# Graph attention on one core: transposed-square transfers per group of four units instead of per slot, with mixing a slot later and the projections re-timed

## The chip, the cores and the metric

The kernel runs on one core of a Trainium2 chip. The metric is device time in microseconds (us) of one execution. Besides the timed runs there is one profiled execution of the kernel before, from which all rows below are taken.

## What is computed

Eight batches of 1024 tokens with 384 features go through masked attention with six heads of 64 features, an output projection, a residual and a layer norm. All arithmetic is fp32.

```python
q = _heads(x @ Wq + bq); k = _heads(x @ Wk + bk); v = _heads(x @ Wv + bv)
scores = jnp.einsum('bhqd,bhkd->bhqk', q, k) / np.sqrt(64)
bias = jnp.where(adj, 0.0, -9e15)[:, None]
probs = jax.nn.softmax(scores + bias, axis=-1)
ctx = jnp.einsum('bhqk,bhkd->bhqd', probs, v)
out = _layernorm(x + ctx.reshape(8, 1024, 384) @ Wf + bf)
```

## The kernel before

**Units, slots, groups.** A unit is one head against one tile of 128 queries: 128 x 1024 scores. A slot holds two units, the two heads of a pair for the same query tile. A batch has 24 slots. A group is two consecutive slots (four units: two query tiles, called qt 0 and 1, of one pair of heads); a batch has 12 groups, and three groups (six slots) finish 256 queries.

**The way of one slot s.** TensorE (PE) computes the scores in line 503 from `q_hi`, `q_lo`, `k_hi`, `k_lo` (three products of fp32r halves stand for one fp32 product) into `score_ps`, which holds one slot only. VectorE (DVE) adds the mask and takes the row minimum of the negated scores (line 689), writing `prob`. ScalarE (ACT) takes the exponential and the row sum (line 611). DVE transposes 32x32 blocks inside `prob` (line 697). What is left of the transposition of the 128x1024 probabilities is a move of 32-partition strips between partitions, and DMA does that: `move_square` (line 301) copies one strip a, c from `prob` to `prob_t`. There are 16 strips: SyncE (SP) issues the 12 with a different from c, ACT issues the 4 others. When both slots of a group have landed, PE mixes: `mix` (line 519) multiplies `prob_t` with `v_all` into `context_ps`. DVE multiplies the result with the spread inverse sums (`divide`, line 707), ACT makes `context_hi`, GpSimd (POOL) makes `context_lo`.

**The table `STEADY`.** Everything else is a job in a written table, slot by slot. Its letters: x transposes the input of the next batch, k, q and v are projections, i spreads the inverse sums of a group (line 439), m mixes a group, p is an output projection of a tile of 128 tokens (lines 408 to 410). In ("q", 2, 1, 0) the numbers are the pair, the 256 queries and the batch ahead. On PE a slot is: scores of s, then its jobs in the order of the table. On ACT: two exponentials, evictions of the jobs, the four DMA issues, `context_high`. On DVE: two maskings, two transposes, `divide`, inverse sums, then for each p `add_residual` and `moments`. On POOL: the low halves of x, k and q (`low_part`, line 812), the next mask, `make_diagonal` for the next group (line 818), `context_low`, `residual` (line 801), `normalise` (lines 839 to 843, 294). Each engine runs its own list in order and waits on semaphores.

**What ties the engines.** The scores of slot s+1 wait until slot s is masked. Jobs share three banks of `job_ps`: a job waits until the job three before it has been evicted, and evictions stand behind the exponentials of their slot. The masking of a slot waits until its part of `prob` has landed in `prob_t`; `prob` has three slots (`RING = 3`). `prob_t` has two groups; the moves of a group wait until the group two before it is mixed. `context_high` reuses one of six `context_hi` buffers. The first scores of a pair wait for the low halves of its q:

```python
def scores(b, s):
    group, pair, qt = s // 6, s % 6 // 2, s % 2
    pe.wait_ge(masked, at(b, UNITS, 2 * s + 2))
    if qt == 0:
        for kind, piece in (("k", 1), ("q", group)):
            if kind == "k" and group:
                continue
            pe.wait_ge(lo_done, needed(b, kind, pair, piece))
```

Six further tables say in which slot SP stores and loads (`STORES`, `RES_LOADS`, `X_LOADS`) and POOL adds `bf` and normalises (`RESIDUALS`, `NORMALISE`).

Of the kernel before, what the change touches and what calls it, by code (L numbers as in the profile page):

```python
# [14 lines left out]
P = 128  # L15
# [7 lines left out]
SLOTS = 24  # L23
RING = 3
# [34 lines left out]
LAST_22 = [("p", 4, 0, 0), ("p", 5, 0, 0)]  # L59
LAST_24 = [("i", 11, 0, 0), ("m", 11, 0, 0), ("p", 6, 0, 0), ("p", 7, 0, 0)]  # L60
# [5 lines left out]
STORES = {5: -2, 12: -1, 16: 0, 20: 1}  # L66
RES_LOADS = {8: 2, 15: 3, 19: 0, 23: 1}
X_LOADS = {2: (0, 0), 4: (0, 1), 11: (1, 0), 14: (1, 1)}
RESIDUALS = {1: 0, 2: 1, 11: 2, 17: 3}
NORMALISE = {3: -2, 10: -1, 13: 0, 18: 1}  # L70
# [14 lines left out]
def slot_work(mode, s):  # L85

    if s >= SLOTS:
        return LAST_24 if mode == "last" else []
    if mode == "first" and s < 2:
        return FIRST_0 if s == 0 else FIRST_1  # L90
    if mode == "last" and s == 22:
        return LAST_22
    return [w for w in STEADY[s] if not (mode == "first" and w[1] < 0) and not (mode == "last" and w[3] == 1)]


def slots_of(mode):
    return range(SLOTS + 1 if mode == "last" else SLOTS)
# [8 lines left out]
def graph_attention(nc, x, adj, wq, bq, wk, bk, wv, bv, wf, bf, out):  # L106
# [15 lines left out]
    with ExitStack() as ctx:  # L122
# [16 lines left out]
        res = sb("res", [P, TT, H], F32)  # L139
# [7 lines left out]
        context_hi = sb("context_hi", [P, 2 * FT, GQ], F32R)  # L147
        context_lo = sb("context_lo", [P, 2 * FT, GQ], F32R)
# [5 lines left out]
        row_min = sb("row_min", [P, 2 * RING], F32)  # L154
# [14 lines left out]
        bv_wide = prob[:, RING - 1, 3].rearrange("p h n -> p (h n)")[:, 0:FT * P].rearrange("p (t n) -> p t n", t=FT)  # L169
# [14 lines left out]
        res_loaded = [sem(f"res_loaded{g}") for g in range(4)]  # L184
# [6 lines left out]
        landed = [sem(f"landed{i}") for i in range(RING)]  # L191
# [22 lines left out]
        stored = [sem(f"stored{g}") for g in range(4)]  # L214
# [95 lines left out]
        def _(sp):  # L310
# [6 lines left out]
            for g in (2, 3):  # L317
                sp.dma_start(res[:, 2 * g:2 * g + 2, :], x_tiles[0, :, 2 * g:2 * g + 2, :]).then_inc(res_loaded[g], 16)
# [8 lines left out]
            sp.dma_start(bf_rows[:], bf.partition_broadcast(P)).then_inc(bf_in, 16)  # L327
            for g in range(2):
                sp.dma_start(res[:, 2 * g:2 * g + 2, :], x_tiles[0, :, 2 * g:2 * g + 2, :]).then_inc(res_loaded[g], 16)
            for i in range(RING):  # L330
                sp.sem_inc(landed[i], 256)
# [7 lines left out]
            def move(b, s):  # L339
                sp.wait_ge(squared, at(b, UNITS, 2 * s + 2))  # L340
                if s % 2 == 0:
                    sp.sem_inc(sp_waited, 1)
                    sp.wait_ge(mixed, at(b, GROUPS, s // 2 + 1))
                for a in range(4):
                    for c in range(4):
                        if not (a == c):
                            move_square(sp, s, a, c)
# [12 lines left out]
            def load_residual(b, group, ahead):  # L360
                sp.wait_ge(stored[group], at(b, 16, 16 * ahead))
# [544 lines left out]
```

## Time and profile before

| | |
|---|---|
| timed runs | 1724.23, 1729.52, 1731.74 us, median 1729.52 |
| the profiled execution | 1730.58 us, of which the span of the instructions is 1728.6 |
| busy in the span | PE 77%, DVE 61%, ACT 42%, POOL 38% |
| mean granted clock of TensorE | 0.881 of full speed |
| DMA | 251.61 MB, mean 146 GB/s |

Busy time counts no DMA issues. What SP does shows only in the chain that ended last, in its waits and in its timeline.

### The profile page before, as it was taken

Reading aid. Unit: us, or ns where it says so; the run is one execution under the profiler, and the core shown is the slowest. Engines: PE = TensorE matmul, PEld = TensorE weight load, DVE = VectorE, ACT = ScalarE, POOL = GpSimd, SP = SyncE. Lnnn points to the kernel's source line nnn. Section 1 sums busy time; section 2 is a strip of 40 time slices with the busy share of each in tenths; the row PEclk is TensorE's granted clock in tenths of the full one; section 3 lists DMA queues with packets and bytes.
Section 4 is the critical chain, followed back from the end, with each engine's and each line's share of the span. In section 5 each row is a group of like instructions: output and inputs, shape, how many; then the busy total and the mean of one; then the engine's idle time right before and its main releaser. Section 6 shows DMA issues by size and latency. Waiting matters only on the chain.

```text
span 1728.6 us, 29185 instructions
## 1 busy us (share of the span) xinstructions
PE 1326.2 (77%) x8406; PEld 948.2 (55%) x8406; DVE 1060.2 (61%) x1617; ACT 721.8 (42%) x1404; POOL 655.7 (38%) x958
## 2 busy tenths in 40 slices
PE   7777887777877689677897688866887778888773
PEld 5555565545745457455574455644656545565542
DVE  5566665765656656565566765566656567566752
ACT  5444543444434444344443434434443435443430
POOL 2223542444414444154432543325433245333333
PEclk9888898889988889897998888988899889998877
DMA  4556655565455655555555555565555555555552
GB/s 152 141 132 154 159 143 147 150 160 153 121 152 147 163 147 131 147 150 155 147 136 152 149 151 141 138 156 152 149 145 138 154 153 150 153 133 153 149 144 74
DMA packets 184872, 251.61 MB, mean 146 GB/s; under 512 B 52464, under 2 KB 86384, under 8 KB 184688
## 3 DMA queue, kind: packets, MB, share of 16 engines
q1 hardware_dynamic: 147824, 199.06, 44.1%
q10 hardware_dynamic: 36864, 50.38, 11.9%
q8 instruction: 80, 1.31, 0.4%
q14 instruction: 104, 0.85, 0.2%
HBM read 35.33 MB, written 12.58 MB: 28 GB/s over the span
## 4 chain that ended last, share of the span: by engine, by line
SPq 79%; issue 9%; PE 4%; ACT 2%; DVE 2%; DMA 2%; ACTq 1%; POOL 1%; POOLq 0%; DVEq 0%
SPq L301 76%; PE context_ps L519 2%; DMA prob_t<-prob 1%; ACT prob L611 1%; DVE prob L697 1%; ACTq L301 1%; SPq L371 1%; PE score_ps L503 1%; SPq L357 1%; SPq L336 1%; SPq L364 1%; PE job_ps L408 0%; DMA x_in<-in_x_dram 0%; POOL res L294 0%; DVE weight_lo L758 0%
## 5 line engine op out<-in xcount | busy, mean ns | idle before, releaser
L519 PE MATMUL context_ps<-prob_t,v_all 128*64 128x256 f32 x3072 | 468.4, 472 | 239.8 <-DMA prob_t<-prob 239.8
L611 ACT ACTIVATE prob<-prob,row_min 128x1024 f32<-128x1024 f32 x384 | 439.5, 1146 | 500.1 <-DVE row_min L689 433.6
L689 DVE CUSTOM_DVE_ANT_0 prob<-score_ps,mask 128x1024 f32<-128x1024 f32 x384 | 454.3, 1220 | 206.1 <-PE score_ps L503 168.4
L697 DVE STREAM_TRANSPOSE prob<-prob 128x1024 f32<-128x1024 f32 x384 | 457.9, 1231 | 148.9 <-ACT prob L611 148.9
L519 PEld LDWEIGHTS context_ps<-prob_t,v_all 128*64 128x64 f32 x3072 | 294.6, 173 | 413.8 <-issue 298.3
L818 POOL TENSOR_TENSOR diag<-ident,inv_sum 128x512 f32<-128x512 f32 x96 | 99.9, 1040 | 410.5 <-DVE inv_sum L702 408.8
L619 ACT ACTIVATE context_hi<-context 128x256 fp32r<-128x256 f32 x96 | 40.1, 418 | 456.1 <-DVE context L707 285.2
L812 POOL TENSOR_TENSOR q_lo<-raw,q_hi 128x256 fp32r<-128x256 f32 x95 | 69.4, 730 | 351.0 <-ACT raw L603 350.9
L707 DVE TENSOR_TENSOR context<-context_ps,context 128x256 f32<-128x256 f32 x96 | 40.0, 416 | 238.1 <-PE context_ps L519 237.9
L408 PE MATMUL job_ps<-xt_hi,weight_hi 128*128 128x256 f32 (+1 forms) x423 | 149.4, 353 | 26.9 <-ACT raw L601 26.7
L503 PE MATMUL score_ps<-k_hi,q_hi 64*128 64x512 f32 x768 | 145.0, 456 | 21.8 <-DVE row_min L689 16.4
L410 PE MATMUL job_ps<-xt_hi,weight_lo 128*128 128x256 f32 (+1 forms) x423 | 137.2, 324 | 0.0
L409 PE MATMUL job_ps<-xt_lo,weight_hi 128*128 128x256 f32 (+1 forms) x423 | 137.0, 324 | 0.0
L503 PE MATMUL score_ps<-k_lo,q_hi 64*128 64x512 f32 x768 | 123.8, 400 | 0.0
L503 PE MATMUL score_ps<-k_hi,q_lo 64*128 64x512 f32 x768 | 122.2, 395 | 0.0
L408 PEld LDWEIGHTS job_ps<-xt_hi,weight_hi 128*128 128x128 f32 x423 | 81.0, 191 | 74.0 <-issue 36.7
L439 PE MATMUL job_ps<-diag,ones 128*64 128x256 f32 x384 | 68.2, 436 | 52.3 <-POOL diag L818 52.3
L294 POOL TENSOR_SCALAR res<-res,mean_var,inv_dev 128x384 f32<-128x384 f32 x64 | 105.0, 1647 | 6.9 <-POOL inv_dev L843 6.9
L824 POOL TENSOR_TENSOR context_lo<-context,context_hi 128x256 fp32r<-128x256 f32 x96 | 70.5, 735 | 95.2 <-ACT context_hi L619 94.7
L503 PEld LDWEIGHTS score_ps<-k_hi,q_hi 64*128 64x128 f32 x768 | 59.4, 192 | 84.8 <-issue 61.8
L812 POOL TENSOR_TENSOR k_lo<-raw,k_hi 128x512 fp32r<-128x512 f32 x46 | 58.3, 1287 | 110.4 <-ACT raw L603 110.4
L410 PEld LDWEIGHTS job_ps<-xt_hi,weight_lo 128*128 128x128 f32 x423 | 81.3, 192 | 6.7
(72 smaller groups left out, 1717.7 us busy)
## 6 DMA issues: line engine op xcount, KB each, us to landing
prob_t<-prob SPq DMA_DIRECT2D x2304, 64.0 KB, 2.0
prob_t<-prob ACTq DMA_DIRECT2D x768, 64.0 KB, 2.1
res<-in_x_dram SPq DMA_DIRECT2D x32, 384.0 KB, 3.7
out_dram<-res SPq DMA_DIRECT2D x32, 384.0 KB, 2.5
x_in<-in_x_dram SPq DMA_DIRECT2D x30, 384.0 KB, 3.5
adj_in<-in_adj_dram SPq DMA_DIRECT2D x31, 256.0 KB, 2.8
prob_t<-in_L_gnn_Wk_dram SPq DMA_DIRECT2D x1, 576.0 KB, 3.9
prob_t<-in_L_gnn_Wq_dram SPq DMA_DIRECT2D x1, 576.0 KB, 7.8
```

Of the source, the lines that this page charges most:

```text
L294: engine.tensor_scalar(res[:, n, :], res[:, n, :], mean_var[:, group % 2, tile, 0:1], inv_dev[:, group % 2, tile:tile + 1], ALU.subtract, ...
L301: queue.dma_start(prob_t[32 * c:32 * c + 32, group % 2, qt, a].rearrange("p h n -> p (h n)"), prob[32 * a:32 * a + 32, ring, c].rearrange( ...
L408: pe.matmul(dst, left_hi, right_hi, start=(t == 0), stop=False)
L409: pe.matmul(dst, left_hi, right_lo, start=False, stop=False)
L410: last = pe.matmul(dst, left_lo, right_hi, start=False, stop=(t == FT - 1))
L503: last[head] = pe.matmul(score_ps[:, head, keys], q_part[rows, pair, q], k_part[rows, pair, keys], start=(n == 0), stop=(n == 2))
L519: last = pe.matmul(context_ps[64 * head:64 * head + 64, 0:GQ], v_all[:, kt, col:col + HS], keys, start=(kt == 0), stop=(kt == TT - 1))
L611: nc.scalar.activation(probabilities(t), probabilities(t), ACT.Exp, scale=-1.0, bias=row_min[:, ring:ring + 1], accum_out=row_sum[:, s // ...
L689: nc.vector.tensor_tensor_reduce(probabilities(t), in_quarters(score_ps[:, head, :]), in_quarters(mask[:, s % 2, :]), 1.0, HUGE, ALU.add, ...
L697: nc.vector.transpose(probabilities(t), probabilities(t)).then_inc(squared, 1)
L812: nc.gpsimd.tensor_tensor(lo, copy[:, 0:width], hi, ALU.subtract).then_inc(lo_done, 1)
L818: nc.gpsimd.tensor_tensor(diag[:], ident[:].unsqueeze(1).to_broadcast([P, 4, P]), inv_sum[:, group % 2, :].unsqueeze(2).to_broadcast([P, 4 ...
```

## The change

- `prob` becomes [partition, 2 groups, 4, 2 query tiles, 2 heads, 256], and `prob_t` [partition, 2 groups, 4, 2 query tiles, 2 heads, 256] with the query tile inside. So a strip of one group is 32 partitions with one run of 4 KB each. `move_square` takes a group: 16 issues for two slots where 32 stood. `move` stands in odd slots only, and waits for all four units of the group.
- The masking of a slot waits for landed data in even slots only, four slots after the buffer was last filled.
- Mixing moves: groups 0 to 3 from slots 5, 6, 7, 9 to 6, 8, 9, 10; groups 4 to 9 one slot later, to 12, 14, 16, 18, 20, 22; groups 10 and 11 to slots 0 and 2 of the next batch (from 23 and 1). Projections stand mostly in odd slots.
- `res` shrinks from 8 tiles to 4, `context_hi` and `context_lo` from 6 buffers to 4, with other waits on `stored`, `projected` and `res_loaded`. `context_high` of group g now waits for the projections that read group g-4.
- The last batch has two slots of leftovers instead of one.

```diff
 STEADY = {
-    12: [("q", 1, 2, 0), ("p", 1, 0, 0)],
-    13: [("i", 5, 0, 0), ("m", 5, 0, 0)],
-    14: [("q", 2, 2, 0)],
-    15: [("i", 6, 0, 0), ("m", 6, 0, 0)],
+    12: [("i", 4, 0, 0), ("m", 4, 0, 0)],
+    13: [("q", 1, 2, 0), ("p", 1, 0, 0)],
+    14: [("i", 5, 0, 0), ("m", 5, 0, 0)],
+    15: [("q", 2, 2, 0), ("q", 0, 3, 0), ("p", 2, 0, 0)],
...
-RESIDUALS = {1: 0, 2: 1, 11: 2, 17: 3}
-NORMALISE = {3: -2, 10: -1, 13: 0, 18: 1}
+RESIDUALS = {2: -1, 10: 0, 14: 1, 20: 2}
+NORMALISE = {0: -2, 8: -1, 14: 0, 18: 1}
...
-        prob = sb("prob", [P, RING, 4, 2, GQ], F32)
-        prob_t = sb("prob_t", [P, 2, 2, 4, 2, GQ], F32)
+        prob = sb("prob", [P, 2, 4, 2, 2, GQ], F32)
+        prob_t = sb("prob_t", [P, 2, 4, 2, 2, GQ], F32)
...
-        def move_square(queue, s, a, c):
-
-            group, qt, ring = s // 2, s % 2, s % RING
-            queue.dma_start(prob_t[32 * c:32 * c + 32, group % 2, qt, a].rearrange("p h n -> p (h n)"),
-                            prob[32 * a:32 * a + 32, ring, c].rearrange("p h n -> p (h n)")
-                            ).then_inc(landed[ring], 16)
+        def move_square(queue, group, a, c):
+
+            queue.dma_start(prob_t[32 * c:32 * c + 32, group % 2, a].rearrange("p q h n -> p (q h n)"),
+                            prob[32 * a:32 * a + 32, group % 2, c].rearrange("p q h n -> p (q h n)")
+                            ).then_inc(landed[group % 2], 16)
...
-            def move(b, s):
-                sp.wait_ge(squared, at(b, UNITS, 2 * s + 2))
-                if s % 2 == 0:
-                    sp.sem_inc(sp_waited, 1)
-                    sp.wait_ge(mixed, at(b, GROUPS, s // 2 + 1))
+            def move(b, group):
+                sp.wait_ge(squared, at(b, UNITS, 4 * group + 4))
+                sp.sem_inc(sp_waited, 1)
+                sp.wait_ge(mixed, at(b, GROUPS, group + 1))
...
-                for s in (2 * group, 2 * group + 1):
-                    pe.wait_ge(landed[s % RING], at(b, 256 * SLOTS // RING, 256 * (s // RING + 2)))
+                pe.wait_ge(landed[group % 2], at(b, 128 * GROUPS, 256 * (group // 2 + 2)))
...
             def context_high(b, group):
                 act.wait_ge(context_done, at(b, GROUPS, group + 3))
-                if group % 3 == 0:
-                    act.wait_ge(projected, at(b, TT, 2 * (group // 3) + 2))
-                nc.scalar.activation(context_hi[:, group % 6, :], context[:], ACT.Copy).then_inc(context_hi_done, 1)
+                act.wait_ge(projected, at(b, TT, 2 * ((group - 4) // 3) + 6))
+                nc.scalar.activation(context_hi[:, group % 4, :], context[:], ACT.Copy).then_inc(context_hi_done, 1)
...
                 if head == 0:
-                    dve.wait_ge(landed[s % RING], at(b, 256 * SLOTS // RING, 256 * (s // RING + 1)))
+                    if s % 2 == 0:
+                        dve.wait_ge(landed[s // 2 % 2], at(b, 128 * GROUPS, 256 * (s // 4 + 1)))
```

Order of instructions on SP, at the head of the loop over the middle batches, slots 0 and 1 of the kernel before. A move of 12 strips is the row that waits and the row x11.

```order
L343 ISA [waits squared]
L301 DMA prob_t<-prob 32x512 [waits mixed]
L301 DMA prob_t<-prob 32x512 x11
L340 REGISTER_ALU
L301 DMA prob_t<-prob 32x512 [waits squared]
...
L336 ISA [waits mask_done]
L336 DMA adj_in<-in_adj_dram 128x2x1024
```

The same place in the changed kernel, slots 0 and 1:

```order
L338 ISA [waits squared]
L298 DMA prob_t<-prob 32x1024 [waits mixed]
L298 DMA prob_t<-prob 32x1024 x11
L330 ISA
L332 ISA [waits mask_done]
L332 DMA adj_in<-in_adj_dram 128x2x1024
```

The move of slot 0 is gone, and that of slot 1 carries 32x1024 elements per issue instead of 32x512.

Order on POOL before, from slot 12 on: the low half of q (pair 1, third 256 queries), in slot 13 the diagonal and `context_lo` around group 5 and `normalise` (its twelve small instructions shortened to the first), in slot 14 the low half of q (pair 2, third 256 queries).

```order
L812 TENSOR_TENSOR q_lo<-raw,q_hi 128x256 [waits job_out]
...
L818 TENSOR_TENSOR diag<-ident,inv_sum 128x512 [waits job_done]
L824 TENSOR_TENSOR context_lo<-context,context_hi 128x256 [waits context_hi_done]
...
L839 TENSOR_TENSOR newton<-inv_dev 128x2 [waits guess_done]
...
L294 TENSOR_SCALAR res<-res,mean_var,inv_dev 128x384 [waits root_ops]
L294 TENSOR_SCALAR res<-res,mean_var,inv_dev 128x384
...
L812 TENSOR_TENSOR q_lo<-raw,q_hi 128x256 [waits job_out]
```

After, from slot 13 on: low half of the same q, in slot 14 diagonal, `context_lo`, `residual`, `normalise`, in slot 15 the low halves of two q.

```order
L798 TENSOR_TENSOR q_lo<-raw,q_hi 128x256 [waits job_out]
...
L804 TENSOR_TENSOR diag<-ident,inv_sum 128x512 [waits job_done]
L810 TENSOR_TENSOR context_lo<-context,context_hi 128x256 [waits context_hi_done]
L787 TENSOR_TENSOR res<-res,bf_rows 128x384 [waits res_loaded1]
L787 TENSOR_TENSOR res<-res,bf_rows 128x384
...
L825 TENSOR_TENSOR newton<-inv_dev 128x2 [waits guess_done]
...
L292 TENSOR_SCALAR res<-res,mean_var,inv_dev 128x384 [waits root_ops]
L292 TENSOR_SCALAR res<-res,mean_var,inv_dev 128x384
L798 TENSOR_TENSOR q_lo<-raw,q_hi 128x256 [waits job_out] x2
```

The residual stands ahead of `normalise` now, and the q of pair 2 is made in slot 15 instead of 14; its scores stay in slot 16.

## Rows read from the trace of the kernel before

**Rows 1.** The page: busy time, share, instructions; the chain that ended last.

```profile
PE 1326.2 (77%) x8406; PEld 948.2 (55%) x8406; DVE 1060.2 (61%) x1617; ACT 721.8 (42%) x1404; POOL 655.7 (38%) x958
...
SPq 79%; issue 9%; PE 4%; ACT 2%; DVE 2%; DMA 2%; ACTq 1%; POOL 1%; POOLq 0%; DVEq 0%
```

**Rows 2.** The page: DMA queue of ACT; issues of the moves, size, time to landing.

```profile
q10 hardware_dynamic: 36864, 50.38, 11.9%
...
prob_t<-prob SPq DMA_DIRECT2D x2304, 64.0 KB, 2.0
```

**Rows 3.** Waits of SP: who for whom, total us, times, longest.

```profile
SPq L369 <- POOL res L294: 22.2, 2, 15.6
```

**Rows 4.** Timeline of SP's queue: start, us, instructions merged.

```profile
916.57 0.38 SPq L357 DMA_DIRECT2D x_in<-in_x_dram  x1
917.06 7.52 SPq L301 DMA_DIRECT2D prob_t<-prob  x12
```

**Rows 5.** Windows of 210 us: busy of PE, PEld, DVE, ACT, POOL, clock, DMA share.

```profile
1110.00:1320.00 210.00, 165.20 (x1050) 117.49 (x1049) 129.27 (x200) 88.44 (x173) 82.97 (x120) 0.89 0.58 148
```

**Rows 6.** Timeline of PE: scores, spread, mix, scores, q, p, scores.

```profile
746.36 0.73 PE L503 MATMUL score_ps<-k_hi,q_hi 64*128 64x512 f32 x4
...
747.95 0.65 PE L439 MATMUL job_ps<-diag,ones 128*64 128x256 f32 x4
750.60 3.67 PE L519 MATMUL context_ps<-prob_t,v_all 128*64 128x256 f32 x32 [2.00 <-DMA prob_t<-prob]
754.20 0.74 PE L503 MATMUL score_ps<-k_hi,q_hi 64*128 64x512 f32 x4
...
755.79 0.39 PE L408 MATMUL job_ps<-xt_hi,weight_hi 128*128 128x256 f32 x1
...
756.98 0.34 PE L408 MATMUL job_ps<-weight_hi,context_hi 128*128 128x384 f32 x1
...
758.64 0.73 PE L503 MATMUL score_ps<-k_hi,q_hi 64*128 64x512 f32 x4
```

**Rows 7.** Timeline of DVE: a masking, the first p, the next masking.

```profile
721.65 1.23 DVE L689 CUSTOM_DVE_ANT_0 prob<-score_ps,mask 128x1024 f32<-128x1024 f32 x1 [1.17 <-PE score_ps L503]
...
726.62 0.52 DVE L714 TENSOR_TENSOR res<-job_ps,res 128x384 f32<-128x384 f32 x1
...
730.14 1.22 DVE L689 CUSTOM_DVE_ANT_0 prob<-score_ps,mask 128x1024 f32<-128x1024 f32 x1 [0.17 <-issue]
```

**Rows 8.** Timeline of ACT: the eviction of a q behind both exponentials.

```profile
725.21 0.45 ACT L596 ACTIVATE q_hi<-job_ps,bias_qk 128x256 fp32r<-128x256 f32 x1
```

**Rows 9.** Timeline of PE and DVE in a slot with five jobs.

```profile
736.97 0.72 PE L503 MATMUL score_ps<-k_hi,q_hi 64*128 64x512 f32 x4
...
738.84 1.23 DVE L689 CUSTOM_DVE_ANT_0 prob<-score_ps,mask 128x1024 f32<-128x1024 f32 x1 [1.16 <-PE score_ps L503]
...
743.51 0.39 PE L408 MATMUL job_ps<-xt_hi,weight_hi 128*128 128x256 f32 x1 [3.43 <-ACT raw L601]
```

**Rows 10.** Timeline of POOL: a q_lo, a residual; start and end of normalise.

```profile
1641.54 0.73 POOL L812 TENSOR_TENSOR q_lo<-raw,q_hi 128x256 fp32r<-128x256 f32 x1 [6.40 <-ACT raw L603]
...
1646.51 1.96 POOL L801 TENSOR_TENSOR res<-res,bf_rows 128x384 f32<-128x384 f32 x2
...
1651.12 0.19 POOL L839 TENSOR_TENSOR newton<-inv_dev 128x2 f32<-128x2 f32 x1
...
1654.88 3.28 POOL L294 TENSOR_SCALAR res<-res,mean_var,inv_dev 128x384 f32<-128x384 f32 x2 [0.22 <-POOL inv_dev L843]
```

**Rows 11.** Timeline of PE: a mix after a long wait.

```profile
783.13 5.18 PE L519 MATMUL context_ps<-prob_t,v_all 128*64 128x256 f32 x32 [5.96 <-DMA prob_t<-prob]
```

**Rows 12.** Head and tail: first scores; last moves of ACT; last mix.

```profile
25.14 0.74 PE L503 MATMUL score_ps<-k_hi,q_hi 64*128 64x512 f32 x4
...
1693.24 2.45 ACTq L301 DMA_DIRECT2D prob_t<-prob  x4
...
1704.54 5.28 PE L519 MATMUL context_ps<-prob_t,v_all 128*64 128x256 f32 x32 [6.70 <-DMA prob_t<-prob]
```

More of the change, by code:

```diff
@@ L23 @@
 SLOTS = 24
-RING = 3
 STEADY = {
[24 rows of a table removed]
[24 rows of a table added]
 }
@@ L87, in slot_work @@
     if s >= SLOTS:
-        return LAST_24 if mode == "last" else []
+        return LAST_24 if s == SLOTS else LAST_25
     if mode == "first" and s < 2:
         return FIRST_0 if s == 0 else FIRST_1
-    if mode == "last" and s == 22:
-        return LAST_22
     return [w for w in STEADY[s] if not (mode == "first" and w[1] < 0) and not (mode == "last" and w[3] == 1)]
 def slots_of(mode):
-    return range(SLOTS + 1 if mode == "last" else SLOTS)
+    return range(SLOTS + 2 if mode == "last" else SLOTS)
 MODES = ("first", "mid", "last")
@@ L183, in graph_attention @@
         x_loaded = [sem(f"x_loaded{i}") for i in range(2)]
-        res_loaded = [sem(f"res_loaded{g}") for g in range(4)]
+        x_early = sem("x_early")
+        res_loaded = [sem(f"res_loaded{i}") for i in range(2)]
         adj_loaded = sem("adj_loaded")
@@ L190, in graph_attention @@
         squared = sem("squared")
-        landed = [sem(f"landed{i}") for i in range(RING)]
+        landed = [sem(f"landed{i}") for i in range(2)]
         inverted = sem("inverted")
@@ L213, in graph_attention @@
         pool_waited = sem("pool_waited")
-        stored = [sem(f"stored{g}") for g in range(4)]
+        stored = [sem(f"stored{i}") for i in range(2)]
         def at(b, per, plus):
@@ L327, in _ @@
             sp.dma_start(bf_rows[:], bf.partition_broadcast(P)).then_inc(bf_in, 16)
+            sp.wait_ge(job_done, 6)
             for g in range(2):
                 sp.dma_start(res[:, 2 * g:2 * g + 2, :], x_tiles[0, :, 2 * g:2 * g + 2, :]).then_inc(res_loaded[g], 16)
-            for i in range(RING):
-                sp.sem_inc(landed[i], 256)
+                sp.sem_inc(landed[g], 256)
             def load_adjacency(b, group):
@@ L346, in move @@
                         if not (a == c):
-                            move_square(sp, s, a, c)
+                            move_square(sp, group, a, c)
             def load_x(b, half, i):
@@ L382, in body @@
                         store(b, STORES[s])
-                    if s in RES_LOADS:
-                        group = RES_LOADS[s]
-                        if group >= 2 and b.mode != "first":
-                            load_residual(b, group, 0)
-                        if group < 2 and b.mode != "last":
-                            load_residual(b, group, 1)
+                    if s in RES_LOADS and (RES_LOADS[s] >= 2 or b.mode != "first"):
+                        load_residual(b, RES_LOADS[s])
             body(Batch("first", 0, 0))
@@ L396, in _ @@
                 store(last, group)
-            for g in range(4):
-                sp.wait_ge(stored[g], 16 * BATCH)
+            for i in range(2):
+                sp.wait_ge(stored[i], 32 * BATCH)
         @block.tensor
@@ L416, in transpose_x @@
                 for i in range(4):
-                    src = x_in[:, i] if mode != "start" or half == 0 else res[:, 4 + i]
+                    src = x_in[:, i] if mode != "start" or half == 0 else res[:, i]
                     last = pe.transpose(bank[:, i * P:(i + 1) * P], src[:, t * P:(t + 1) * P], ident[:])
@@ L448, in project_out @@
                 three_products(job_bank(b.mode, job)[:, 0:H], [
-                    (context_hi[:, 3 * (group % 2) + t, tok], context_lo[:, 3 * (group % 2) + t, tok],
+                    (context_hi[:, (3 * group + t) % 4, tok], context_lo[:, (3 * group + t) % 4, tok],
                      weight_hi[:, 3, t, :], weight_lo[:, 3, t, :]) for t in range(FT)]).then_inc(projected, 1)
@@ L538, in _ @@
                 if n == 3:
-                    for g in (2, 3):
-                        pe.wait_ge(res_loaded[g], 16)
+                    pe.wait_ge(x_early, 16)
                 if n >= 4:
@@ L607, in exponential @@
                 s, head = t // 2, t % 2
-                ring = 2 * (s % RING) + head
+                ring = 2 * (s % 4) + head
                 col = 2 * head + s % 2
@@ L627, in move @@
                         if a == c:
-                            move_square(act, s, a, c)
+                            move_square(act, group, a, c)
             def body(b):
@@ L638, in body @@
                             evict(b, job)
-                    if s < SLOTS:
-                        move(b, s)
+                    if s < SLOTS and s % 2 == 1:
+                        move(b, s // 2)
                     for job in work:
@@ L796, in residual @@
             def residual(b, g):
-                pool.wait_ge(res_loaded[g], at(b, 16, 16))
-                if g >= 2 and b.mode == "first":
-                    pool.wait_ge(job_done, 6)
-                for n in (2 * g, 2 * g + 1):
+                pool.wait_ge(res_loaded[g % 2], at(b, 32, 16 * (g // 2 + 1)))
+                for n in (2 * g % 4, 2 * g % 4 + 1):
                     nc.gpsimd.tensor_tensor(res[:, n, :], res[:, n, :], bf_rows[:], ALU.add).then_inc(res_done, 1)
@@ L823, in context_low @@
                 pool.wait_ge(context_hi_done, at(b, GROUPS, group + 1))
-                nc.gpsimd.tensor_tensor(context_lo[:, group % 6, :], context[:], context_hi[:, group % 6, :],
+                nc.gpsimd.tensor_tensor(context_lo[:, group % 4, :], context[:], context_hi[:, group % 4, :],
                                         ALU.subtract).then_inc(context_lo_done, 1)
@@ L854, in body @@
                         next_mask(b, s // 6 + 1, s % 6 - 4)
-                    if s == 1 and b.mode == "first":
+                    if s == 2 and b.mode == "first":
                         make_diagonal(b, 0)
@@ L862, in body @@
                             context_low(b, job[1])
-                    if s in RESIDUALS:
+                    if s in RESIDUALS and (RESIDUALS[s] >= 0 or b.mode != "first"):
                         residual(b, RESIDUALS[s])
+                    if s == SLOTS:
+                        residual(b, 3)
                     if s in NORMALISE and (NORMALISE[s] >= 0 or b.mode != "first"):
                         normalise(b, NORMALISE[s])
-                    if s == SLOTS and b.mode == "last":
+                    if s == SLOTS:
                         normalise(b, 2)
+                    if s == SLOTS + 1:
                         normalise(b, 3)
```

58 lines of the change are left out of this document (28 added, 30 removed), and 40 rows, old and new, of the table STEADY.

## The prediction

> **What bounds the kernel now.** I read the chain that ended last first: SP's queue holds 79% of it, while the busiest engine is PE at 77% and DVE has 61% [rows 1]. Next, does SP wait? Its longest entry is 22.2 us in two waits in the whole span [rows 3]. So SP issues nearly all the time. Twelve issues of moves take 7.52 us, 0.63 each, after a load that occupies the queue from 916.57 to 917.06 [rows 4]. One batch is 210 us: a window of that length holds 1050 matmuls [rows 5], and one batch has 288 for scores, 384 for mixing, 48 spreads, 24 transposes and 306 in projections, 1050 together. SP's 24 moves of a batch take 24 x 7.6 = 182 us, its 16 loads and stores about 0.9 us each with what surrounds them, 15 us, and some 13 us are issues that took longer and waits: 210. The bound is the number of SP's issues, 8.75 us per slot.
>
> The other engines wait for it. PE had 5.96 us of waiting for a landed group ahead of one mix, and 6.70 ahead of the last [rows 11, 12].
>
> **The issues.** A middle batch keeps 12 moves of 12 issues on SP. If an issue of 128 KB costs what one of 64 KB does, they take 12 x 7.6 = 91 us, with the rest 91 + 15 + 6 = 112 us per batch. Can it? The bound from below is 0.38 us, what the queue is busy with a load of 384 KB in many more runs [rows 4]; from above it is cost by bytes, 1.27 us. I take 0.63: the load is six times as large and its issue is no longer, so bytes don't set it. ACT's four issues stand once per two slots instead of once per slot.
>
> SP is then far from being the bound, and what is late next is the loop of PE, DVE, ACT and POOL. It decides the time, so I add it up.
>
> **PE slot by slot.** From a stretch in which the matmuls ran fast [rows 6]: scores 1.6 us (746.36 to 747.95; 754.20 to 755.79), mix 3.6 (750.60 to 754.20), q 1.2 (755.79 to 756.98), p 1.6 (756.98 to 758.64, with some 0.1 before the scores). A v has the form of a p, 1.6. By columns k is two q's less the start, estimated 2.1, a spread is 0.5, an x 0.5. The scores of the next slot also wait for this slot's masking: the masking begins 1.9 us after the scores (736.97 to 738.84) [rows 9], and two take 2.4 us, so no slot is under 4.3. DVE needs 5.0 us from masking to the end of the transposes (721.65 to 726.62) and 3.5 for two p with moments (726.62 to 730.14) [rows 7]; a divide about 0.4.
>
> A mixing slot costs PE 1.6 + 0.5 + 3.6 = 5.8 and DVE 5.4. The ten pure ones (2, 6, 8, 9, 10, 12, 14, 16, 18, 20) give 58. Slots 0 and 22 have a q too, 6.9 each. Of the others, PE's sum and DVE's: slot 1 4.3 and 5.1, slot 3 6.4 and 5.1, slot 4 7.9, slot 5 6.4, slot 7 5.9 and 8.4, slot 13 4.3 and 7.1, slot 15 5.4 and 6.6, slot 19 5.9, slots 21 and 23 7.5 each. Slots 11 and 17 have five and six jobs for three banks, so the fourth waits for an eviction behind both exponentials. ACT reached a q's eviction 3.6 us after the masking began (721.65 to 725.21) and takes some 0.9 for it [rows 7, 8]. Before, a slot with three x, a q and a p cost 9.4 us (736.97 to 746.36), 3.43 of it that wait [rows 6, 9]. Slot 11 has these jobs, 9.3; slot 17 one more q, 10.1. Slot 4's fourth job waits 0.9 the same way; it is in the 7.9.
>
> PE's sums give 152 us per batch. Taking the longer of PE and DVE in each slot gives 160. The truth lies between, since a slot long on DVE can lend to a mixing slot. I take 156.
>
> **Waits that the new places add.**
> - *POOL behind the late q.* The scores of slot 16 need the low half of the q of pair 2, now made in slot 15. In slot 14 masking begins at 1.9, the transposes end at 6.9, divide, `context_high` and `context_lo` add 0.4, 0.4 and 0.7: 8.4 us into the slot. Then `residual`, 1.96, and `normalise`, 7.0 (1651.12 to 1658.16) [rows 10]: 17.4. The q_lo, 0.73, ends at 18.1, while PE would start slot 16's scores at 5.8 + 6.6 = 12.4. Price 5.7 us. Before, `normalise` stood one slot earlier and that q in slot 14, two slots ahead of its scores.
> - *POOL behind normalise in slot 8.* The two p of slot 7 shift DVE, so `context_lo` of group 1 ends about 10.6 us into slot 8, `normalise` at 17.6, the diagonal for group 3 at 18.7. Its spread in slot 10 is wanted at 14.0. Price 4.6. The data of group 3 comes about then too: its moves wait for mix 1.
> - *ACT in slot 12.* `context_high` of group 4 now waits for the second p, which PE does in slot 13, and the exponentials of slot 13 stand behind it: 1.7 us late. The q of slot 13 then has its low half 8.8 us into the slot, and the scores of slot 14 wait for it; PE alone would be there at 4.4, DVE at 7. Beyond the 156 this is 3.5.
>
> Together 14: 170 us per batch.
>
> **Does the data land in time?** The 12 issues take 7.6 us and the last lands 2.0 us later [rows 2]. The engines moved ACT's 50.38 MB in 11.9% of the span, 245 GB/s; a burst of 2.1 MB needs 8.6 us by that. So a group lands 9.6 to 10.6 us after its transposes. A mix two slots later is wanted some 13 us after them. Hidden, with 3 us to spare, except for groups 2 and 3, whose moves wait for the mixes of 0 and 1 in slots 6 and 8; there masking or mixing waits 0 to 1 us, beside the POOL wait counted. SBUF — State Buffer of the Trainium skill, section "Door 1: The DMA port swizzle", states that 32 partitions reach only 8 of the 16 ports, 218 GB/s. By that rule alone a burst would take 9.6 us and land at 11.6, still under 13, and cost at most 1 us in group 3, 8 us in all. The rows show 245 GB/s for strips of 32 partitions, so I keep that.
>
> **The clock.** At 0.881 granted on average, and 0.89 in a middle batch [rows 5], the clock was at its lower level, 1.2 instead of 2.4 GHz, for a quarter of the time. After a wait of 5.96 us a mix took 5.18 us, after 2.00 us 3.67 [rows 6, 11]. Three waits of 4 to 7 us remain per batch by the list above, against one ahead of most mixes today, so at 1.5 to 2.5 us each about 7. That gives 177 us per batch.
>
> **The sum.** The head is 25 us to the first scores, unchanged. Eight batches are 8 x 177 = 1416. The first lacks two p and two mixes, the last the x, k and q of a next one, worth -16. Before, the last transposes ended at 1693.2, and the span at 1728.6: 35. SP's backlog, which held the last mix until 1704.54 [rows 12], becomes one landing of 10, and `normalise` of group 2 runs ahead, so 31. 25 + 1416 - 16 + 31 = 1456 of span, against 1728.6. The profiled execution took 1730.58, 2 more than its span and 1 over the median of 1729.52. Forecast 1458 us.
>
> **Rivals.**
> - *The added waits don't come about*, since DVE's long slots delay PE anyway: 156 to 162 per batch and less low clock. 25 + 8 x 158 - 16 + 31 = 1304. For it: PE does 138 us of fast matmuls per batch. Against it: the waits are in the order and the durations in the rows. 0.13.
> - *The issue or the landing grows with bytes, in part.* At 1.0 to 1.2 us per issue a burst lands at 14 to 17 us, over the 13, and PE waits 1 to 3 us at most mixes: 183 to 198 per batch, 1510 to 1620. The same holds if PE's clock stays low for 40% of the time. For it: the runs double, both queues ask for 400 GB/s in a burst and get 245. 0.11.
> - *Slower than before: an issue of 4 KB runs costs twice or more.* The place is SP's queue. It decides from 1.27 us per issue, where 144 x 1.27 + 27 = 210 as now; at 1.4 a batch is 229, and the time 1728 + 8 x 19 = 1880. For it speaks nothing but that no row has such an issue. 0.03.
> - *No change*: the cost lies exactly at that point. 0.01.
>
> TensorE: Matmul & The Clock Gate of the Trainium skill, section "Part 1: The HAM clock gate", says that the throttled clock is the default and activity releases it. If a busier PE kept the full level throughout, the sum would lose the 7 us per batch, about 1402, inside my range.
>
> **Chances.** The forecast, 165 to 190 per batch, has 0.72. To leave out 2 in 10, the range goes to 1370 below, past which lies most of the first rival, and to 1560 above, half way through the second. Under 0.5%, 9 us, a measurement of this kernel can't be told from no change. Faster 0.96, same 0.01, slower 0.03.
>
> **What would show it.** Right: SP's queue under 15% of the chain; an issue of 128 KB at 0.55 to 0.65 us; landing within 3 us; PE waiting for POOL's q_lo ahead of one in 24 scores, about 5 us; slots 11 and 17 unchanged in length; DVE and PE sharing the chain. Wrong: issues over 1 us, PE waiting for landed data ahead of most mixes, or a batch near 158 us with no wait for POOL. The prediction fails most likely in the sum of small hand-overs between engines, which I took from few rows.

## The result and the profile after

The changed kernel takes 1574.99 us (median of 4, 1573.23 to 1576.45) against 1727.85 (median of 4, 1724.23 to 1731.74). The ratio is 0.9115, 95% interval 0.9091 to 0.9138: faster by 153 us. The forecast was 1458 us with a range of 1370 to 1560. Direction and bound were right, the time was 117 us too low, and it lies outside the range. Times are of executions in the faster of a kernel's two states; of all the runs below one execution was slow, 1532.95 us of the kernel with one `normalise` later, and it is left out of that kernel's time.

The page of the changed kernel: busy time of each engine, ACT's DMA queue, and the moves (count, size of one, us to landing).

```profile
PE 1277.9 (81%) x8406; PEld 916.7 (58%) x8406; DVE 1058.4 (67%) x1617; ACT 722.5 (46%) x1404; POOL 657.1 (42%) x958
...
q10 hardware_dynamic: 18432, 50.36, 13.1%
...
prob_t<-prob SPq DMA_DIRECT2D x1152, 128.0 KB, 3.6
prob_t<-prob ACTq DMA_DIRECT2D x384, 128.0 KB, 4.0
```

The instruction counts are those of [rows 1]; PE is busy 48 us less, since it runs at the lower clock less often. Half as many moves carry the same bytes [rows 2], and one lands after 3.6 or 4.0 us, not 2.0.

Waits in its trace: who waited for whom, total us, times, longest.

```profile
SPq L337 <- DVE prob L685: 490.4, 96, 23.8
SPq L298 <- PE context_ps L509: 80.6, 23, 5.7
...
DVE prob L685 <- ACT prob L600: 194.1, 192, 8.1
PE score_ps L494 <- POOL q_lo L798: 87.1, 17, 7.3
PE job_ps L431 <- POOL diag L804: 13.6, 7, 2.8
PE context_ps L509 <- DMA prob_t<-prob: 9.9, 2, 7.5
```

SP, whose longest entry was 22.2 us in two waits [rows 3], now waits 571 us for transposes and mixes. PE waits for landed data twice in the span. In the place of SP's queue stand waits between engines; the one to look at is DVE's for the exponentials, 194.1 us, which the forecast has no line for. It is not new, though. The same group on the page of the kernel before:

```profile
L697 DVE STREAM_TRANSPOSE prob<-prob 128x1024 f32<-128x1024 f32 x384 | 457.9, 1231 | 148.9 <-ACT prob L611 148.9
```

A middle batch of the new kernel is 191 us, not 177 (first scores of the batches at 595.4 and 786.2). Fourteen us in each of eight batches are 112 of the 117 that are missing. Its window, columns as in [rows 5]:

```profile
595.40:786.20 190.80, 158.53 (x1050) 113.18 (x1050) 130.54 (x200) 90.03 (x176) 82.99 (x120) 0.91 0.67 163
```

**Slot by slot.** I took the time from the first score matmul of each slot to that of the next, in the six middle batches, and the median of the six. "Forecast" is the prediction's own list, the longer of PE and DVE, with its three waits of POOL and ACT in their places, which comes to 173.8 (before its 7 us for the clock and the 4 that DVE lends).

| slots | forecast | after | difference |
|---|---|---|---|
| 0 to 5 | 38.5 | 44.2 | +5.7 |
| 6 to 9 | 25.8 | 36.2 | +10.4 |
| 10 | 10.4 | 7.6 | -2.8 |
| 11, 12 | 15.1 | 15.0 | -0.1 |
| 13, 14 | 16.4 | 17.0 | +0.6 |
| 15, 16 | 18.1 | 20.1 | +2.0 |
| 17 | 10.1 | 11.2 | +1.1 |
| 18 to 23 | 39.4 | 39.9 | +0.5 |

So most slots stand as worked out, and the place to look at is slots 6 to 9. Timeline of slots 6 to 8 of a middle batch, ACT, DVE, both queues and the mixes 0 and 2:

```profile
641.81 1.22 DVE L677 CUSTOM_DVE_ANT_0 prob<-score_ps,mask 128x1024 f32<-128x1024 f32 x1 [1.45 <-PE score_ps L494]
641.94 3.62 PE L509 MATMUL context_ps<-prob_t,v_all 128*64 128x256 f32 x32
...
645.61 3.73 ACTq L298 DMA_DIRECT2D prob_t<-prob  x4
...
649.45 1.15 ACT L600 ACTIVATE prob<-prob,row_min 128x1024 f32<-128x1024 f32 x1 [8.98 <-issue]
...
650.84 2.38 DVE L685 STREAM_TRANSPOSE prob<-prob 128x1024 f32<-128x1024 f32 x2 [6.65 <-ACT prob L600]
...
652.15 0.44 PE L400 MATMUL job_ps<-weight_hi,context_hi 128*128 128x384 f32 x1 [2.11 <-ACT context L575]
...
662.10 3.75 ACTq L298 DMA_DIRECT2D prob_t<-prob  x4
...
665.96 1.15 ACT L600 ACTIVATE prob<-prob,row_min 128x1024 f32<-128x1024 f32 x1 [8.14 <-issue]
...
670.16 5.36 PE L509 MATMUL context_ps<-prob_t,v_all 128*64 128x256 f32 x32 [1.95 <-DVE context L695]
```

The masking of slot 6 starts at 641.81 and lets the exponential start some 1.25 us later, at 643.1. It starts at 649.45, 6.4 us late. In between ACT's queue waits for mix 0, which ends at 645.56, and then issues four transfers until 649.34. The gap reads "issue", since an engine whose own queue waits for a semaphore shows no releaser; the row of ACTq shows what was in front. The same stands at mix 1: ACTq at 662.10, the exponential of slot 8 at 665.96, 2.7 us late. After that everything is late in turn: transposes by 6.65, the second p of slot 7 by 2.11 (it wants ACT's eviction), mix 2 by 1.95, and that mix then takes 5.36 us for 3.62.

How late ACT starts an exponential behind its masking can be read for every slot. Medians of the six middle batches: 6.4 us in slot 6, 2.7 in slot 8, 2.1 in slot 2, and 1.2, 1.1 and 1.0 in slots 10, 4 and 20, all behind ACT's moves; 1.7 in slot 13, behind `context_high`; under 0.1 us in all others. The kernel before had such a stall too. In its slot 5, in a middle batch, ACT's moves of slot 4 waited for mix 0, and the exponential began 5.2 us behind its masking:

```profile
693.19 2.46 ACTq L301 DMA_DIRECT2D prob_t<-prob  x4
...
695.76 1.15 ACT L611 ACTIVATE prob<-prob,row_min 128x1024 f32<-128x1024 f32 x1 [7.72 <-issue]
```

So the cause stood in the trace on which the forecast was made.

### The profile page after: what moved, and what is told of

Read it like the earlier page. It is cut to its first block and busy times, and to the rows that moved or that the text cites. A ratio compares the mean times of both kernels' runs of the same rounds, so it can differ in the third digit from the quotient of the medians.

```text
span 1574.4 us, 27551 instructions
## 1 busy us (share of the span) xinstructions
PE 1277.9 (81%) x8406; PEld 916.7 (58%) x8406; DVE 1058.4 (67%) x1617; ACT 722.5 (46%) x1404; POOL 657.1 (42%) x958
## 3 DMA queue, kind: packets, MB, share of 16 engines
q10 hardware_dynamic: 18432, 50.36, 13.1%
## 5 line engine op out<-in xcount | busy, mean ns | idle before, releaser
L600 ACT ACTIVATE prob<-prob,row_min 128x1024 f32<-128x1024 f32 x384 | 439.7, 1146 | 595.4 <-DVE row_min L677 439.2
L685 DVE STREAM_TRANSPOSE prob<-prob 128x1024 f32<-128x1024 f32 x384 | 458.0, 1231 | 194.1 <-ACT prob L600 194.1
L509 PE MATMUL context_ps<-prob_t,v_all 128*64 128x256 f32 x3072 | 386.6, 409 | 37.7 <-DVE context L695 27.8
L509 PEld LDWEIGHTS context_ps<-prob_t,v_all 128*64 128x64 f32 x3072 | 241.4, 150 | 177.5 <-issue 71.9
L494 PE MATMUL score_ps<-k_hi,q_hi 64*128 64x512 f32 x768 | 154.1, 481 | 148.8 <-POOL q_lo L798 87.1
L400 PE MATMUL job_ps<-xt_hi,weight_hi 128*128 128x256 f32 (+1 forms) x423 | 145.1, 343 | 0.0
L494 PE MATMUL score_ps<-k_hi,q_lo 64*128 64x512 f32 x768 | 133.0, 425 | 0.0
L494 PE MATMUL score_ps<-k_lo,q_hi 64*128 64x512 f32 x768 | 131.8, 422 | 0.0
L775 POOL TENSOR_SCALAR mask<-adj_in 128x1024 f32<-128x1024 uint8 x64 | 67.1, 1049 | 93.4 <-DVE row_min L677 58.2
L400 PE MATMUL job_ps<-weight_hi,context_hi 128*128 128x384 f32 x192 | 74.3, 387 | 21.9 <-ACT context L575 14.9
L494 PEld LDWEIGHTS score_ps<-k_hi,q_lo 64*128 64x128 f32 x768 | 80.5, 204 | 19.0
L494 PEld LDWEIGHTS score_ps<-k_lo,q_hi 64*128 64x128 f32 x768 | 80.4, 204 | 19.1
```

The costliest lines, as they stand in the source:

```text
L400: pe.matmul(dst, left_hi, right_hi, start=(t == 0), stop=False)
L494: last[head] = pe.matmul(score_ps[:, head, keys], q_part[rows, pair, q], k_part[rows, pair, keys], start=(n == 0), stop=(n == 2))
L509: last = pe.matmul(context_ps[64 * head:64 * head + 64, 0:GQ], v_all[:, kt, col:col + HS], keys, start=(kt == 0), stop=(kt == TT - 1))
L600: nc.scalar.activation(probabilities(t), probabilities(t), ACT.Exp, scale=-1.0, bias=row_min[:, ring:ring + 1], accum_out=row_sum[:, s // ...
L685: nc.vector.transpose(probabilities(t), probabilities(t)).then_inc(squared, 1)
```

## The experiments

The explanation to be tested: **ACT's issues for groups 2 and 3 wait for mixes 0 and 1, and the exponentials of slots 6 and 8 are queued behind them.** Its rivals: the transfers themselves are late (a burst lands later than forecast), or POOL's waits cost more than was counted. Each expectation names its own theories, A first. All ratios are against the kernel before on the same chip, whose medians there were 1724.93 us (first four) and 1725.21 us (last four). These lie 3 us under the 1727.85 beside which the changed kernel was timed, so that differences in us between kernels are good to some 3 us.

**ACT's issues of groups 2 and 3 behind the exponentials.**

```diff
+LATE_MOVES = (2, 3)
-                    if s < SLOTS and s % 2 == 1:
+                    if s < SLOTS and s % 2 == 1 and s // 2 not in LATE_MOVES:
                         move(b, s // 2)
+                    if s < SLOTS and s % 2 == 0 and s // 2 - 1 in LATE_MOVES:
+                        move(b, s // 2 - 1)
```

> Edit: in ACT's list the four issues of groups 2 and 3 stand after the exponentials and evictions of the next slot (6 and 8), not ahead of them; nothing else moves. Theory A (the missing time of slots 6 to 9 is ACT's: its issues wait for mix 0 and mix 1, and the exponentials queue behind them, 6.4 and 3 us late): the transposes of slot 6 end some 7 us after its scores begin instead of 13.4, slots 7 to 9 together shrink from 30 us to 21 to 25, and the kernel takes 1575 - 8 x 6 to 8 x 9, 1505 to 1530 us. Theory B (landing is the limit there: groups 2 and 3 land 13 us after mixes 0 and 1 whatever ACT does, since landing takes 3.6 us and not 2.0): masking of slots 8 and 10 then waits for the DMA instead, and the gain is under 3 us per batch, 1550 to 1575 us.

Measured: 1517.23 us (1512.62 to 1519.43), ratio 0.879 (0.8767 to 0.8812), 58 us under the changed kernel. Its slot 6, and PE in its slot 10:

```profile
618.81 1.15 ACT L601 ACTIVATE prob<-prob,row_min 128x1024 f32<-128x1024 f32 x1 [2.61 <-DVE row_min L680]
...
620.20 2.39 DVE L688 STREAM_TRANSPOSE prob<-prob 128x1024 f32<-128x1024 f32 x2 [0.28 <-ACT prob L601]
...
621.35 3.74 ACTq L299 DMA_DIRECT2D prob_t<-prob  x4
...
647.95 0.65 PE L432 MATMUL job_ps<-diag,ones 128*64 128x256 f32 x4 [4.43 <-POOL diag L807]
...
648.44 5.31 PE L510 MATMUL context_ps<-prob_t,v_all 128*64 128x256 f32 x32
```

The same four transfers now stand behind the exponentials, and the transposes wait 0.28 us where they waited 6.65. Slot 7 falls from 10.5 to 6.0, slot 9 from 11.6 to 6.7. Slot 10 grows from 7.6 to 11.8: PE waits 4.43 us for POOL's diagonal, at the place and near the 4.6 us that the forecast gave. In the changed kernel ACT's stall had covered it. Theory A holds. ACT's smaller delays, in slots 2, 4 and 20, are left as they were, and one of 1.1 us is new in slot 7.

**All sixteen issues on SP**, none on ACT.

```diff
-                        if not (a == c):
-                            move_square(sp, group, a, c)
+                        move_square(sp, group, a, c)
...
-                    if s < SLOTS and s % 2 == 1:
-                        move(b, s // 2)
```

> Edit: all 16 issues of a group on SP, none on ACT. Theory A (ACT's waiting and its 3.0 to 3.7 us of issuing per group hold back exponentials in every odd slot; SP has 40% of its time free): exponentials of slots 6 and 8 are on time, odd slots lose up to 1 us; the group lands 3 us later, at 15 us after its transposes, which eats part: 1500 to 1545 us. Theory B (landing time binds): mixes and maskings wait for the DMA, 1570 to 1640 us.

Measured: 1496.56 us (1494.77 to 1502.01), ratio 0.8683 (0.8662 to 0.8703), 78 us under the changed kernel and below what A gave. Its page and SP's queue:

```profile
prob_t<-prob SPq DMA_DIRECT2D x1536, 128.0 KB, 2.4
```

```profile
664.65 11.12 SPq L298 DMA_DIRECT2D prob_t<-prob  x16
...
678.73 10.07 SPq L298 DMA_DIRECT2D prob_t<-prob  x16
```

Sixteen issues alone take 10.07 to 11.12 us, 0.63 to 0.70 each, and land after 2.4. That is about the forecast's issue price; beside ACT's queue it was not met. Slots 6 to 9 come to 27.4 us (forecast 25.8), and slots 0 to 5 fall from 44.2 to 40.4, since ACT now starts its exponentials on time in every slot but 13. That is why this edit gives more than the one before. The last data of a group lands 12.4 us after the group's first issue, where it took 11.4 (medians of the middle batches). DVE pays 39.3 us for landed data, and it is still the better kernel.

**The new table with transfers of 64 KB**, on the two queues as after, twice as many issues.

```diff
-            queue.dma_start(prob_t[32 * c:32 * c + 32, group % 2, a].rearrange("p q h n -> p (q h n)"),
-                            prob[32 * a:32 * a + 32, group % 2, c].rearrange("p q h n -> p (q h n)")
+            for qt in range(2):
+                queue.dma_start(prob_t[32 * c:32 * c + 32, group % 2, a, qt].rearrange("p h n -> p (h n)"),
+                                prob[32 * a:32 * a + 32, group % 2, c, qt].rearrange("p h n -> p (h n)")
```

> Edit: the changed kernel's table and buffers, but each strip goes in two issues of 64 KB with runs of 2 KB, so 32 issues per two slots as before. Theory A (SP's issue count was the bound and its halving is the whole gain): SP again issues all the time, 24 x 7.6 + 15 + waits for the moves that now come in one block per group, so 1730 to 1850 us, no faster than before. Theory B (the later mixing and the odd-slot projections brought a good part of the 153 us): 1600 to 1700 us.

Measured: 1785.68 us (1777.74 to 1790.12), ratio 1.0332 (1.0305 to 1.036). Chain by engine, two waits, and the moves:

```profile
SPq 64%; PE 14%; issue 10%; ACTq 4%; DVE 3%; ACT 2%; DMA 1%; POOL 1%; DVEq 0%; POOLq 0%
```

```profile
DVE prob L678 <- DMA prob_t<-prob: 158.4, 47, 7.4
PE context_ps L510 <- DMA prob_t<-prob: 111.4, 29, 9.9
```

```profile
prob_t<-prob SPq DMA_DIRECT2D x2304, 64.0 KB, 2.0
prob_t<-prob ACTq DMA_DIRECT2D x768, 64.0 KB, 2.1
```

The new table and buffers, with one move for a whole group, cost 3.3% by themselves; only with half the issues does the change win, and it then wins 211 us over this version. The gain is the count of issues, as forecast. The old table with large transfers was not run.

**`normalise` of the first 256 queries and its store one slot later** (out of the way of the q_lo that slot 16 needs).

```diff
-STORES = {4: -2, 10: -1, 16: 0, 20: 1}
+STORES = {4: -2, 10: -1, 17: 0, 20: 1}
-NORMALISE = {0: -2, 8: -1, 14: 0, 18: 1}
+NORMALISE = {0: -2, 8: -1, 15: 0, 18: 1}
```

> Edit: normalise of group 0 (of 256 queries) in slot 15 behind the low halves of q, instead of in slot 14 ahead of them; its store one slot later, in 17. Theory A (slot 15's 11.6 us are POOL's: the q_lo that the scores of slot 16 need waits behind normalise): slot 15 falls to 7 to 8 us, slot 16 loses its slow mix too (8.5 to 6), 1575 - 8 x 5 to 8 x 6.5, 1523 to 1535 us. Theory B (ACT's eviction of that q is late anyway): under 2 us per batch, 1560 to 1575.

Measured: 1515.51 us (1503.58 to 1517.5), ratio 0.882 (0.8769 to 0.887): 59 us under the changed kernel by the median times, 51 by the ratios, with 9 us of uncertainty. The wait in the changed kernel, a row of its timeline, and what all waits for q_lo come to in this one (87.1 before the edit):

```profile
725.95 1.41 POOL L798 TENSOR_TENSOR q_lo<-raw,q_hi 128x256 fp32r<-128x256 f32 x2
726.73 1.22 PE L494 MATMUL score_ps<-k_hi,q_hi 64*128 64x512 f32 x4 [5.99 <-POOL q_lo L798]
```

```profile
PE score_ps L494 <- POOL q_lo L798: 49.3, 17, 4.4
```

The forecast had 5.7 us for this wait; it is 5.99. Slot 15 falls from 11.6 to 7.1 and slot 16 from 8.5 to 5.6, 7.4 together: the wait, and the slow matmuls behind it (scores 1.22 for 0.74). Theory A. The profiled execution is the fastest of this kernel, so that its slots show the gain at its largest; that the gain exceeds what A gave is not clear of the scatter.

**Both together.** All issues on SP, and `normalise` of the first 256 queries later, in one kernel.

```diff
-                        if not (a == c):
-                            move_square(sp, group, a, c)
+                        move_square(sp, group, a, c)
+STORES = {4: -2, 10: -1, 17: 0, 20: 1}
+NORMALISE = {0: -2, 8: -1, 15: 0, 18: 1}
```

> Edit: all 16 issues on SP and normalise of group 0 in slot 15 with its store in 17, together. Theory A (two separate stalls, ACT's queue in slots 6 to 9 and POOL's in 14 to 16): the gains of 78 and 58 us add, less what one median hides, 1430 to 1450 us. Theory B (both take up the same slack of one loop): no better than the better of the two, 1480 to 1500 us.

Measured: 1445.55 us (1444.48 to 1450.92), ratio 0.8372 (0.8352 to 0.8391). Alone the edits are worth 78 and 51 to 59 us, together 129: a sum within the scatter, two separate costs.

**Then `normalise` of the last 256 queries of the batch before one slot later too.**

```diff
-STORES = {4: -2, 10: -1, 17: 0, 20: 1}
+STORES = {4: -2, 11: -1, 17: 0, 20: 1}
-NORMALISE = {0: -2, 8: -1, 15: 0, 18: 1}
+NORMALISE = {0: -2, 9: -1, 15: 0, 18: 1}
```

> Edit: as e5_sp_and_normalise, and normalise of group 3 (of the batch before) in slot 9 instead of 8, its store in 11. Theory A (slot 10's 10.6 to 11.8 us in the kernels without ACT's stall are PE waiting for the diagonal of group 3, behind normalise on POOL, 4.6 us by the prediction): slot 10 falls to 6 to 7 us, 25 to 35 us less than e5_sp_and_normalise. Theory B (slot 10 waits for group 3's data, whose moves wait for mix 1): within 10 us of e5_sp_and_normalise, and the trace shows PE's mix waiting for the DMA there.

Measured: 1422.44 us (1420.08 to 1423.78), ratio 0.8235 (0.8215 to 0.8256), 23 us less. Slot 10 falls from 11.6 to 6.8, the 4.8 us of the diagonal. Slots 2 and 14 give back 1.6 and 1.0 of it, so the gain is a little under A's.

**Then `context_high` and `context_lo` of group 4 behind slot 13's work.**

```diff
-                        if job[0] == "m":
+                        if job[0] == "m" and job[1] != 4:
                             context_high(b, job[1])
+                    if s == 13:
+                        context_high(b, 4)
```

POOL has the same edit with `context_low(b, 4)`.

> Edit: as e6_normalise_9, and context_high and context_low of group 4 in slot 13 behind the evictions and low halves, instead of in slot 12 ahead of the exponentials of 13. Theory A (the 1.7 us by which slot 13's exponentials are late carry to the scores of slot 14, 8.8 us into the slot): slot 13 falls from 8.8 to 7.1 us, 10 to 18 us less than e6_normalise_9. Theory B (the q of slot 13, made one slot ahead of its scores, sets it alone): under 5 us.

Measured: 1405.29 us (1399.84 to 1405.4), ratio 0.813 (0.8105 to 0.8155), 17 us less: slot 13 from 8.8 to 7.2, and slots 14 and 2 give back the 1.0 and 1.6 that they had grown by in the run before (slot 4 grows by 1.4). This was the forecast's third wait. A window of 168 us of this kernel, its DVE waits and its chain:

```profile
600.00:768.00 168.00, 148.80 (x1060) 108.76 (x1056) 131.49 (x201) 91.22 (x179) 83.06 (x120) 0.98 0.77 186
```

```profile
DVE prob L684 <- ACT prob L599: 53.9, 192, 0.6
DVE prob L676 <- DMA prob_t<-prob: 44.1, 20, 3.4
```

```profile
PE 56%; issue 15%; SPq 12%; ACT 6%; DVE 5%; DMA 3%; POOL 2%; DVEq 0%; ACTq 0%; POOLq 0%
```

It is the fastest version of the study, 18.7% under the kernel before and 10.8% under the changed one. PE is what is left. It is busy 148 us with a batch's matmuls, where the changed kernel needs 159, at a granted clock of 0.98 there.

**The mixes back in the odd slots**, with the large transfers (of groups 5 to 9, spread and mix at the end of the slot before).

```diff
-    15: [("q", 2, 2, 0), ("q", 0, 3, 0), ("p", 2, 0, 0)],
-    16: [("i", 6, 0, 0), ("m", 6, 0, 0)],
+    15: [("q", 2, 2, 0), ("q", 0, 3, 0), ("p", 2, 0, 0), ("i", 6, 0, 0), ("m", 6, 0, 0)],
+    16: [],
```

> Edit: the changed kernel with spread and mix of groups 5 to 9 one slot earlier, at the end of the odd slots 13 to 21; all else as it is. Theory A (a group lands 12 to 13 us after its transposes, with 3.6 us of landing, so mixing a slot earlier meets data that are 1 to 5 us late): PE waits for the DMA ahead of five mixes per batch, 8 x 5 x 2 to 8 x 5 x 4 more, 1650 to 1730 us. Theory B (the mixes' place is nearly free once the issues are halved, since PE reaches them only behind the odd slots' projections): 1550 to 1610 us.

Measured: 1614.02 us (1608.34 to 1615.37), ratio 0.9344 (0.9314 to 0.9374), 39 us over the changed kernel.

```profile
DVE context L695 <- PE context_ps L509: 180.2, 45, 12.7
PE context_ps L509 <- DMA prob_t<-prob: 11.9, 3, 9.3
PE score_ps L494 <- POOL q_lo L798: 4.6, 8, 2.7
```

Theory A, that the mixes would wait for landed data, fell: PE waits for it 11.9 us in three waits. The loss is in the full odd slots, 17 (15.5 for 11.2), 19 (12.2 for 6.0) and 21 (11.6 for 7.6). There the mix stands behind all projections, and DVE's `divide`, and with it what DVE has next, waits for it, 180.2 us where it was 27.2. The even slots 14, 16, 20 and 22, now without a mix, win back 3.5, 3.8, 1.2 and 2.2 us. Part of that has another cause: PE's waits for q_lo fall from 87.1 to 4.6 us, so the 39 us are what is left after a second stall is gone. So in this kernel the mix's new place is not needed for the data's sake. That its gain is that the two kinds of slot are level fits these rows, but no run separates it from the waits for q_lo.

## Why the prediction was right and where it was wrong

**The bound and what removed it: right.** SP's queue was the bound, and its issues halved freed it; with the same table and issues of 64 KB it holds 64% of the chain again.

**The step that failed** stands in "Does the data land in time?": moves of groups 2 and 3 "wait for the mixes of 0 and 1 in slots 6 and 8; there masking or mixing waits 0 to 1 us". It asked when the data lands and not what stands behind the waiting issues. On SP only other transfers are queued behind them. On ACT the exponentials of the next slot are: in both kernels ACT's moves stand at the end of a slot, ahead of them. The forecast had at most 8 us for these waits in the whole span. Putting the issues of groups 2 and 3 behind the exponentials gave 58, taking all issues off ACT 78. In batches: 10 of the 14 us that a middle batch is too long are gone then (191.1 to 180.9), and the other 4 are in the terms below. The Trainium skill says of the other way to issue a DMA, from GpSimd, in DMA: Bandwidth & Descriptors, section "Anatomy of one DMA — SWDGE (gpsimd) path": "any semaphore wait happens on the issuing sequencer before dispatch". The trace agrees for ACT's issues, with 6.4 us at the first of the two.

**The added waits: right in place, near in size.** POOL behind the late q: 5.7 forecast, 5.99 measured. POOL behind `normalise` in slot 8: 4.6 and 4.43, but visible only once ACT's stall was gone, so the changed kernel does not pay for it in full (at most 2.8 us per wait). ACT in slot 12: 3.5 forecast; PE waited 4.29 for the q_lo ahead of slot 14. Slot 13 took the 8.8 us that the forecast's own account gives; what was not counted is that slot 14 then took 8.2 instead of 5.8, its mix 3.70 to 4.80 us instead of 3.62. Undoing the three waits gave 51 to 59, 23 and 17 us. The rival without them, 1304 us, is excluded; with all of them and ACT's stall gone the kernel takes 1405. Its "138 us of fast matmuls per batch" has no row: at a granted clock of 0.98 they took 148. In the second wait the spread is put at 14.0 us, where 5.8 + 5.8 + 1.6 of the forecast's own list give 13.2.

**Terms mis-sized.** Slots 0 to 5 were 5.7 us short. Of these 3.8 are the failed step again, since they go when ACT issues nothing: in slot 2 the exponentials were 2.1 us late. In slot 4 I took 7.9 us for the fourth job's wait behind the exponentials; the slot takes 10.3, and 8.3 to 9.9 in the six faster versions (11.3 before). In slot 0 the masking begins 5.8 us after the scores and not 1.9; of a wait of 3.68 us ahead of it the profile names no releaser. And the 4 us that a slot long on DVE was to lend don't exist: slots 7 and 8 take 6.0 and 7.9 with ACT's issues late, 13.9 together, where the longer of PE and DVE gives 14.2 and PE alone 11.7. So 160 was the right base, not 156.

**Issue and landing: too low, and hidden.** In the middle batches of the changed kernel twelve issues take 8.4 to 10.6 us (median 8.7), not 7.6, and land after 3.6, not 2.0. One of the longer moves:

```profile
690.54 9.63 SPq L298 DMA_DIRECT2D prob_t<-prob  x12
692.15 3.79 ACTq L298 DMA_DIRECT2D prob_t<-prob  x4
```

A group has landed 10.8 to 12.5 us (median 11.4) after its issues began, not 9.6 to 10.6. That is still under the 13 at which it was wanted, and PE waits only 9.9 us in two waits. The rival of a size-dependent price had 1.0 to 1.2 us per issue and 14 to 17 to landing; 0.72 and 11.4 were measured. That its 1510 to 1620 holds the measured time is luck: ACT's queue did it. By SBUF — State Buffer, section "Door 1: The DMA port swizzle", of the Trainium skill, 32 partitions reach 218 GB/s. ACT's strips of 32 partitions moved 50.36 MB in 13.1% of 1574.4 us, 244 GB/s, as before. This is a rate by the packet time of all 16 engines with strips of other partitions in flight, so it neither shows nor refutes the page's figure for one strip, and the forecast's 9.6 us for a whole burst by that figure took the strips of a burst to share one limit, which no run shows.

**The clock: right in direction, a little low in size.** The window is at 0.91 against 0.89 [rows 5], so it hardly recovers while waits remain. With four of them gone it is 0.98, and PE is busy 148 us a batch instead of 158.5. That is over 10 us of slower matmuls, where the forecast had 7; how much of it delays the batch was not measured. The rule of TensorE: Matmul & The Clock Gate, section "Part 1: The HAM clock gate", in the Trainium skill, that activity releases the throttled clock, agrees with the 0.98 there; the change alone raised it by 0.02 only.

**What would show it.** The chain view of the changed kernel follows only a few per cent of its span, so "SP under 15%" can't be read from it; in the fastest version it is 12%. The other signs: an issue of 0.55 to 0.65 us came only with SP alone (0.72 in the changed kernel), landing within 3 us did not come (3.6), the wait for q_lo of some 5 us came (5.99), and slots 11 and 17 took 9.4 and 11.2 us for 9.3 and 10.1.

**Open:** why both queues together raise issue and landing times was not taken apart further; and what holds the masking of slot 0, and what slot 4 takes beyond its list, have no run of their own.

## What to carry to other kernels

When a change makes a DMA issue wait for a later event, list what stands behind that issue on its own engine, for each queue that issues a part of the group. Look for it in the trace before the change: a compute engine that is idle with "issue" and has its own queue's row right ahead of it. A compute engine that issues transfers pays with its compute; once the dedicated queue has room, put the issues there (78 us here), even though the data lands 1 us later. And where a stall covers another, the second appears when the first is taken away: slot 10 went from 7.6 to 11.8 us, so work through the list until each has been undone.

## What the runs showed of the hardware that was not expected

- **Two queues that issue at once slow each other with transfers of 128 KB, and not with 64 KB.** In the changed kernel an issue on SP took 0.80 us in the mean while ACT issued too and 0.65 while it did not, and one on ACT 0.80; with all on SP it is 0.63. With 64 KB it is 0.61 to 0.64 on SP either way, in the kernel before as with the new table. Landing took 3.6 and 4.0 us for 128 KB with both, 2.4 alone, and 2.0 and 2.1 for 64 KB with both.
- **With SP alone, an issue of 128 KB costs about what one of 64 KB does** (0.63 in the mean; 0.63 [rows 4]).
- **A mix of 32 matmuls after a wait of only 2 us took 5.36 us for 3.62**; before, one after 2.00 us took 3.67 [rows 6]. The clock had fallen earlier there: behind a wait of 2.37 us the scores ahead of that mix took 1.08 us for four matmuls instead of 0.73, at a granted clock of 0.54, near its lower level. A wait's length alone did not tell which of the two clock levels the matmuls behind it got.
